# A gated cross-attention block with an FP8 feed-forward on one core: the attention stage's work dealt out anew, and the first hidden tile done in halves

## The reference

```python
q = c @ Wq.T + bq;  k = c @ Wk.T + bk
attention = softmax(q @ k.T)                       # per batch, 256 x 256
x  = x + tanh(g_xattn) * einsum('bln,bmn->blm', layernorm(x), attention)
h  = layernorm(x)                                  # rounded to e4m3
a  = gelu(h @ w_gating[0]) * (h @ w_gating[1])     # rounded to e4m3
x  = x + tanh(g_ffn) * (a @ w_linear)
```

## Time and profile before

| | before |
|---|---|
| median of 3 runs | 49.53 us |
| the profiled execution | 49.46 us |
| its span | 47.7 us |
| TensorE matmul busy | 41.9 us (88%) |
| VectorE | 34.5 us (72%) |
| ScalarE | 29.4 us (62%) |
| GpSimd | 17.0 us (36%) |
| chain that ended last: TensorE | 63% |
| the same: VectorE | 12% |
| the same: DMA | 10% |

### The profile page before, as it was taken

How to read it: one execution, slowest core, us unless ns; L and a number is a source line. 1 busy time by engine, 2 the same in 40 slices (tenths; PEclk the granted TensorE clock), 3 DMA queues, 4 the chain that set the end, 5 groups by cost and what they waited for, 6 DMA issues and landing times.

```text
span 47.7 us, 831 instructions
## 1 busy us (share of the span) xinstructions
PE 41.9 (88%) x242; PEld 28.4 (60%) x242; DVE 34.5 (72%) x108; ACT 29.4 (62%) x66; POOL 17.0 (36%) x35
## 2 busy tenths in 40 slices
PE   3999999963999999998999999999999999999000
PEld 1327888824788888772436555756565588863000
DVE  0103639999797979799999990987666999589700
ACT  0642937399897899655699749765555874563000
POOL 3200799039999550600700250000000599002300
PEclk9999999999999999999999999999999999999999
DMA  0499899999999970000000000000000015330092
GB/s 0 61 361 335 308 368 401 340 189 136 89 103 105 105 73 1 0 0 21 0 0 0 0 0 0 0 0 7 0 0 0 0 54 173 112 115 0 0 340 101
DMA packets 3604, 4.64 MB, mean 97 GB/s; under 512 B 400, under 2 KB 2320, under 8 KB 3600
## 3 DMA queue, kind: packets, MB, share of 16 engines
q1 hardware_dynamic: 2448, 3.61, 22.0%
q0 software_dynamic: 864, 0.79, 18.1%
q10 hardware_dynamic: 288, 0.20, 1.3%
HBM read 5.90 MB, written 1.05 MB: 146 GB/s over the span
## 4 chain that ended last, share of the span: by engine, by line
PE 63%; DVE 12%; DMA 10%; SPq 3%; issue 2%; ACT 2%; DVEq 1%
PE bank L640 14%; PE bank L600 14%; PE bank L646 14%; PE bank L665 13%; DMA x_sb<-x 10%; DVE st L415 4%; PE bank L572 4%; DVE nmax L422 2%; PE bank L622 2%; PE bank L565 2%; SPq L209 2%; DVE mv L418 1%; DVE attn L433 1%; ACT xq L349 1%; DVE yo L488 1%
## 5 line engine op out<-in xcount | busy, mean ns | idle before, releaser
L473 DVE SCALAR_TENSOR_TENSOR ap<-bank,gl 128x512 f16<-128x512 f32 (+1 forms) x19 | 11.5, 603 | 3.8 <-PE bank L646 2.2
L358 ACT ACTIVATE gl<-bank 128x512 bf16<-128x512 f32 (+1 forms) x19 | 9.8, 525 | 5.6 <-PE bank L640 5.5
L640 PE MATMUL bank<-xq,wg 128*128 128x512 fp8e4 (+1 forms) x38 | 10.0, 346 | 0.2 <-ACT xq L349 0.2
L646 PE MATMUL bank<-xq,wg 128*128 128x512 fp8e4 (+1 forms) x38 | 10.0, 346 | 0.0
L665 PE MATMUL bank<-wl,aq 128*128 128x256 fp8e4 x64 | 9.7, 273 | 0.1
L665 PEld LDWEIGHTS bank<-wl,aq 128*128 128x128 f16 x64 | 6.1, 98 | 3.5 <-DVE aq L482 0.6
L600 PE MATMUL bank<-attnT,xT_sb 128*128 128x256 f32 x32 | 8.1, 385 | 0.0
L278 POOL TENSOR_TENSOR yo<-ys,x 128x256 f32<-128x256 f32 x4 | 3.0, 776 | 9.3 <-ACT ys L366 9.3
L263 POOL TENSOR_TENSOR r<-ve,neg_half 128x2 f32<-128x2 f32 x4 | 3.0, 759 | 8.5 <-DVE ve L456 8.5
L600 PEld LDWEIGHTS bank<-attnT,xT_sb 128*128 128x128 f32 x32 | 5.6, 190 | 0.7 <-ACT attnT L332 0.2
L482 DVE TENSOR_SCALAR aq<-ap 128x512 uint16<-128x512 uint16 (+1 forms) x19 | 5.7, 302 | 0.0
(11 more groups left out here) (50 smaller groups left out, 54.7 us busy)
## 6 DMA issues: line engine op xcount, KB each, us to landing
x_sb<-x SPq DMA_DIRECT2D x4, 256.0 KB, 4.7
xT_sb<-xT SPq DMA_DIRECT2D x4, 256.0 KB, 5.9
out<-yo SPq DMA_DIRECT2D x6, 128.0 KB, 2.1
wg<-w_gating POOLq DMA_DIRECT2D x4, 128.0 KB, 8.7
par<-params_ctxT SPq DMA_DIRECT2D x1, 256.0 KB, 4.4
wl<-w_linear POOLq DMA_DIRECT2D x2, 128.0 KB, 8.7
out<-yo SPq DMA_DIRECT2D x1, 256.0 KB, 2.0
par<-params_ctxT SPq DMA_DIRECT2D x1, 192.0 KB, 2.7
```

The costliest lines, as they stand in the source:

```text
L358: nc.scalar.activation(gl[:, s % 2, toks], gate_b[s % 2][:, toks], ACT.Gelu_apprx_tanh).then_inc(gelu_ready, 1)
L473: nc.vector.scalar_tensor_tensor(ap[:, s % NAP, toks], up_b[s % 2][:, toks], ACT_SCALE, gl[:, s % 2, toks], ALU.mult, ALU.mult).then_inc(p ...
L640: mm = nc.tensor.matmul(gate_b[s % 2][:, toks], wg8[:, c, k, 0, o:o + P], xq[:, g, k, toks], start=(k == 0), stop=(k == KC - 1))
L646: mm = nc.tensor.matmul(up_b[s % 2][:, toks], wg8[:, c, k, 1, o:o + P], xq[:, g, k, toks], start=(k == 0), stop=(k == KC - 1))
```

## The change

The computation stays the same. What is dealt out or ordered anew:

- *kT and the normalisation.* `k_out` moves from ScalarE to VectorE (a `tensor_scalar` addition). `normalise` is done by GpSimd for all four batches, and `turn_attention` waits tile by tile.
- *Early energies and maxima.* TensorE does energy(1) before the third and fourth projections, and VectorE takes each maximum before the statistics of the later batches, which are scattered between.
- *Scales per pair.* `scales1(h)` makes s1 for two batches at a time; the row constants nms1 come later (`shifts1`).
- *x2 without its row constant.* `add_attention` adds the plain x. The constant, which the second layer norm takes out anyway, is added at the end: in `scale_out` as the bias (per tile now), and for the last three tiles by `shift_x2` on ScalarE into x2s.
- *norm2.* Batches 0, 2 and 3 on ScalarE (`ACT_NORM`), batch 1 on VectorE.
- *First hidden tile in halves.* The first step is split in two, one batch each, so there are 20 steps; the first waits for batch 0's xq alone. `X_AFTER` goes from (3, 6) to (5, 7). x2 of batch 3 and its statistics stand between the first products on VectorE.

The diff, cut to its core. In order: the steps; GpSimd's scales and its list of calls; VectorE's new `k_out` and `add_attention`; ScalarE's loop over the steps; VectorE's loop; the wait of ffn2's first matmul (unchanged); TensorE's first calls.

```diff
-    STEPS = [divmod(n, HT) + (0, GB) for n in range(G * HT - SPLIT)]
+    STEPS = [(0, j, i, i + 1) for i in range(GB) for j in range(FIRST)]
+    STEPS += [divmod(n, HT) + (0, GB) for n in range(FIRST, G * HT - SPLIT)]
-    X_AFTER = (3, 6)
+    X_AFTER = (5, 7)
+    ACT_NORM = (0, 2, 3)
...
+            def scales1(h):
+
+                pair = slice(h * B // 2, (h + 1) * B // 2)
+                pool.wait_ge(mv1_ready, LT * (h + 1) * B // 2)
+                nc.gpsimd.tensor_scalar(ve1[:, pair], mv1[:, pair, :, 1], EPS, None, ALU.add).then_inc(ve1_ready, 1)
+                nc.gpsimd.tensor_tensor(r1[:, pair], ve1[:, pair], neg_half[:, pair], ALU.pow).then_inc(r1_ready, 1)
+                nc.gpsimd.tensor_scalar(s1[:, pair], r1[:, pair], tg[:, 0:1], None, ALU.mult).then_inc(s1_ready, 1)
...
-            scales1()
-            shift_x(0)
-            shift_x(1)
-            normalise(B - 1)
+            normalise(0)
+            normalise(1)
+            scales1(0)
+            normalise(2)
+            normalise(3)
+            scales1(1)
             for b in range(B):
                 rstd2(b)
+                if b == 1:
+                    shifts1()
...
+            def k_out(b):
+                dve.wait_ge(k_done, b + 1)
+                nc.vector.tensor_scalar(kT[:, b * L:(b + 1) * L], k_b[b % 2][:, 0:L], bk, None,
+                                        ALU.add).then_inc(k_ready, 1)
...
-                    nc.vector.scalar_tensor_tensor(x2[:, b, t], halves(pv_b[b % 2])[:, t], s1[:, b, t:t + 1], xs[:, b, t],
-                                                   ALU.mult, ALU.add).then_inc(x2_ready, 1)
+                    nc.vector.scalar_tensor_tensor(x2[:, b, t], halves(pv_b[b % 2])[:, t], s1[:, b, t:t + 1],
+                                                   x_sb[:, b, t], ALU.mult, ALU.add).then_inc(x2_ready, 1)
...
             for s in range(S):
                 gelu(s)
-                if s == X_AFTER[0] - 2:
+                if s == X_AFTER[0] - 1:
                     norm2(2)
-                if s == X_AFTER[1] - 2:
+                if s == X_AFTER[1] - 1:
                     norm2(3)
...
+                if X_AFTER[1] < s <= X_AFTER[1] + LT + 1:
+                    shift_x2(s - X_AFTER[1] - 1)
...
-                if s == 1:
-                    stats2(B - 1, 0)
-                    stats2(B - 1, 1)
-                if s == 2:
-                    moments2(B - 1)
+                if s == 0:
+                    stats2(2, 1)
+                if s == 1:
+                    add_attention(3, [0])
+                if s == 2:
+                    add_attention(3, [1])
+                    moments2(2)
+                if s == 3:
+                    stats2(3, 0)
+                if s == 4:
+                    stats2(3, 1)
+                if s == 5:
+                    moments2(3)
...
                 if s == 0:
                     pe.wait_ge(x2_ready, LT * B)
...
             energy(0)
+            energy(1)
             project_q(2)
             project_k(2)
-            energy(1)
             project_q(3)
```

More of the change, by code:

```diff
@@ L197, in flamingo_block @@
         s_out = sem("s_out")
+        first_of_g1 = next(s for s, step in enumerate(STEPS) if step[0] == 1)
         def last_step(b):
@@ L588, in turn_attention @@
                     pe.wait_ge(q_ready, B)
-                turn(turn_b[b % 2], attn[:, b]).then_inc(attn_turned, 1)
+                for t in range(LT):
+                    pe.wait_ge(pool_attn_ready, LT * b + t + 1)
+                    for k in range(KC):
+                        mm = nc.tensor.transpose(halves(turn_b[b % 2])[:, k, t * P:(t + 1) * P],
+                                                 attn[:, b, t, k * P:(k + 1) * P], ident[:, :])
+                mm.then_inc(attn_turned, 1)
             def attend(b, parts=tuple(pairs(range(LT), range(KC)))):
@@ L693, in _ @@
             attend(3, [(1, 1)])
+            ffn1(0)
             for s in range(S):
-                ffn1(s)
+                if s > 0:
+                    ffn1(s)
                 if LAG <= s < S - HOLD:
```

206 lines of the change are left out of this document (93 added, 113 removed).

## The result

The changed kernel took 50.73 us in the median of 4 runs (50.18 to 51.22), against 49.53 before (4 runs, 49.49 to 49.55): 1.021 times the time, 95% interval 1.012 to 1.030. It is slower, as forecast (50.05, range 49.4 to 50.7 us), but by about 1.2 us in the median of all four, just beyond the upper end of the range, and by 1.0 us by the ratio, just inside it; forecast were 0.5. The profiled execution is the longest of the four: 51.22 us with a span of 49.4, against 49.46 and 47.7.

A forecast was written before the change was run, and what follows sets the result against it. TensorE, almost without a break from 11.44 to about 41.9 us, was taken as the bound. Head -1.57, waits +1.04 and +1.20, an earlier stall -0.05 gave +0.61 on 49.46: 50.07, stated as 50.05 us, range 49.4 to 50.7.

The forecast's parts named there:

- First transposes "at 10.33": Head, TensorE: after three energies and the projections, batch 0's attention transposes can start at 10.33, against 11.44 before.
- The first FFN matmul then starts at 20.55.: End of the head: 9.99 us of TensorE work from 10.33 plus 0.25 stall; 20.55 instead of 22.12, 1.57 gained.
- a first FFN matmul after 21.2: Sign that the forecast is wrong: then rival 2 holds, and GpSimd's rows say which instruction.
- rival 2: GpSimd makes the head late, at the second scales1 and batch 0's power before X0: +0.85, 50.9 us; chance 0.12.
- the power of 128x4 1.07: GpSimd's second scales1 in the head: not in the trace, taken as 1.07 between 128x8 (1.68) and 128x2 (up to 0.82).
- the other estimate: GpSimd normalisation by the Trainium skill's factor of two: 0.62 a tile, the whole about 50.6 us.
- It waits 1.04: First ffn2 matmul: TensorE stands at 23.15, x2 of batch 3 is complete at 24.15, so it waits 1.04 to 24.19.
- 1.2 us more: At X3, batch 3's x2 transposes: TensorE loses 1.2 us in two waits (0.8, 0.4) for ScalarE's xh tiles.
- VectorE then sits idle about 2 us. That costs nothing more.: At product(7): gelu(7) queues behind the waiting xh on ScalarE; VectorE idles, but TensorE needs it one step later.
- The last stretch is edit for edit as before ... Zero.: From the matmul behind X3 to the end: no change in time, since x2s is ready long ahead.
- the first (waits covered): Rival 1: FFN waits covered, earlier head kept; 47.84 us without stalls, 48.9 with the first alone; chance 0.13, everything under 49.43.
- The third (the two cancel): Rival 3: head gains 0.1 more, chain 0.5 shorter, nothing left of +0.61; 49.43 to 49.63 us; chance 0.08.

The follow-up runs named there:

- The warm-up runs: Warm-up matmuls cut from six to one: in the kernel before, 49.80 us, ratio 1.006; in the changed kernel with x2 and statistics early, 50.14 us.

## Why the prediction was right, and what was mis-sized

The mechanism was right at each step, and the sum was short of the measured one: +0.61 forecast, +1.76 between the two profiled executions (51.22 - 49.46), +1.2 between the medians and +1.0 by the ratio. Half of the difference in the traces is a term that the sum did not have (the second point below).

- *First transposes "at 10.33".* They stood at 11.12. 0.57 of the 0.79 is the later first energy. The other 0.22 lies between it and the transposes (4.79 us instead of 4.57): the first two energies took 2.15 us to the next projection, where 1.77 is what they take in one piece, so the wait for kT(1) cost 0.38 instead of 0.28; the two energies without it took 1.77 instead of 1.72, and the third energy took 0.91 (10.21 to 11.12) instead of 0.86.
- *"The first FFN matmul then starts at 20.55."* It stood at 21.30. From the first transposes on it is 10.18 us, forecast 10.22. With an unshifted start, in the run with x2 alone early, it stood at 20.46. The step that failed is one that had no term: that the projections start at full clock. The page says so in all 40 slices, and so it does after the change; but the rows do not. A product at the start is 0.85 to 1.01 us from the next in place of 0.43, one before the change and two after it. With 0.12 of a later first matmul (3.56 against 3.44) this is the whole 0.57. I read the page's line where I should have read the start-to-start times of the first rows. The warm-up runs show what that is worth: hidden up to 1.30 us in the old head, passed on for the most part by the new one. It also spoiled a sign: "a first FFN matmul after 21.2" was to mean rival 2, and 21.30 came without it.
- *kT 0.47, the power of 128x4 1.07, "GpSimd makes the head late".* kT took 0.45 to 0.48, the power 1.04, a normalised tile on GpSimd 0.47 (two in 0.94 at 9.63, in the trace) and not the 0.62 of the other estimate. The line between the neighbouring sizes held, and rival 2 did not occur: no wait of TensorE before the first FFN matmul names GpSimd.
- *"It waits 1.04" at ffn2.* The row says 1.03, but it counts from the end of the record before; the forecast counts from start to start, and so read TensorE lost 1.20: it could have started at 24.03 (the up projection begins at 23.60 and costs 0.43) and did at 25.23. Two terms were too small. VectorE's product(0) started 0.94 behind the first FFN matmul instead of 0.83, which left x2 complete at +3.68 (24.98) instead of +3.60; and TensorE took up its work 0.25 us behind x2's end instead of 0.04. Against that it came to the wait 0.13 later than forecast, since the third up projection had to wait 0.12 for product(0) to free its bank (product(0) ended at 22.66, the matmul started at 22.73).
- *"1.2 us more" at X3.* From the first ffn2 matmul to the matmul behind X3 it took 6.72 us (25.23 to 31.95), forecast 6.85 (24.19 to 31.04). The order of releases was the one forecast: power and `nmr` on GpSimd to 30.65, `xh` at 30.68, X3 at 31.42. With the step before, the stretch is 10.65 instead of 10.49.
- *"VectorE then sits idle about 2 us. That costs nothing more."* Row 32.34 has 2.00. Nothing is lost behind it: the stretch from there differs by 0.18 us, and a wait of that size stands at the tail, next point.
- *"The last stretch is edit for edit as before ... Zero."* It was +0.18. `scale_out` in four activations puts GpSimd's additions beside other roundings. Before the change two roundings were lengthened:

```profile
37.55 0.83 DVE L482 TENSOR_SCALAR aq<-ap 128x512 uint16<-128x512 uint16 x1
...
39.46 0.46 DVE L482 TENSOR_SCALAR aq<-ap 128x512 uint16<-128x512 uint16 x1
```

  After it three are, 0.71, 0.73 and 0.48. The one that starts at 40.47 ends at 41.20, and the ffn2 pair that needs it starts at 41.26, 0.42 behind the start of the half up projection at 40.84 in place of 0.22. These 0.20 us are, within the rounding of the spans, the 0.18 of the stretch. I had looked at whose instructions are the same, not at what runs beside them. No experiment took the additions away altogether. The Trainium skill (SBUF — State Buffer, Who interferes with whom) has VectorE and GpSimd share a port pair as an exclusive lock, which a VectorE `tensor_scalar` may take in its two-port mode; the roundings, three of which can be seen above to end 0.08 to 0.15 us behind an addition's end, agree with that, and the product, which reads one operand from PSUM, stayed at 0.69 throughout. No trace shows the port itself.

Of the rivals, the first (waits covered) was what one reordering makes true: with x2 and the statistics early, the median is 48.6 to 48.7, between the 47.84 and 48.9 that the rival gave. For the order that the change has, it was out of the question, as argued: VectorE's idle 1.27 us before product(0) could not be used by work that stands behind product(1). The third (the two cancel) had a head and a chain shorter than the sum; both came out longer.

Three things stay open. Why the same six warm-up matmuls are followed by one slow product in one execution and by three in the next was not found, nor whether the change has a part in it; starts can be read only in the profiled executions, one for each run. On the later chips the kernel before scattered too (48.91 to 51.17 us), with no trace to say why. And that the halves are worth nothing rests on one trace without them and on the mean clocks, not on the medians.

## What to carry to other kernels

An engine that works in order is idle where its next instruction waits, not where you would like it to be: work that others need soon belongs ahead of the wait, and here moving x2 and the statistics ahead of the first product was worth 2.0 us. Two waits of one engine in a row are not two prices, since removing the first lets it arrive earlier at the second, so trace the later chain to its own source before pricing either. When a change removes slack ahead of the busiest engine, what the slack used to hide (here up to 1.30 us of a slow start) is passed on, so price that too.

## What the runs showed of the hardware

- TensorE's first fp32 products can run at half speed, 0.85 to 1.02 us per pair of records instead of 0.43, although the page's granted clock reads full. Behind the same six warm-up matmuls none is slow in two traces (0.50 to 0.64 from start to start; first energy at 5.72 and 5.76), one to three are in the others, and in two of these a part of the fourth (first energy at 6.79 and 6.91); behind a single warm-up matmul all four and some of the energy after them.
- A 16-bit rounding of 512 columns on VectorE, 0.28 us alone, lasts up to 0.71 to 0.83 when it starts while GpSimd adds 128x256 fp32 (0.72 each where one stands alone), and ends 0.08 to 0.15 us behind the end of an addition.
- From the end of the work waited for to the start of what waited, it took 0.03 us from GpSimd's `nmr` to ScalarE's `xh`, 0.07 and 0.08 from VectorE's variance to GpSimd's power, 0.14 from ScalarE's gelu(0) (end 22.10) to VectorE's product (22.24), and 0.25 from VectorE's x2 to TensorE's ffn2. It does not follow the length of the wait: those engines had waited 1.34, 5.03 and 3.04, 1.27 and 1.03 us. The forecast had 0.03 to 0.08 for all.
- GpSimd's power costs 0.70 to 0.82 us for 128x2, 1.04 for 128x4 and 1.68 for 128x8 (0.82 and 1.68 in the earlier trace rows, 0.70 and 1.04 after the change): a line of about 0.16 us per column over a base of 0.4.
